# Local attention's product with V in four tiles of 64x64, its result in two banks, and one plain copy of the turned weights

## What is computed

```
bq = q.reshape(b, h, nw, w, d)                  # w = 32, nw = 8 windows, d = 64
bk2, bv2 = (look(bk), look(bv))                 # keys of the window before and of this one: 64
mask = (it < jb) | (it > jb + w) | (jb == -1)
sim = jnp.einsum('bhwie,bhwje->bhwij', bq, bk2) * QK_SCALE
sim = jnp.where(mask, -jnp.finfo(sim.dtype).max, sim)
attn = jax.nn.softmax(sim, -1)
out = jnp.einsum('bhwij,bhwje->bhwie', attn, bv2)
```

## Time and profile before

| | us |
|---|---|
| median of three runs | 1871.23 |
| lowest and highest | 1869.65, 1872.12 |
| the profiled execution's own time | 1873.87 |
| its span, first to last instruction | 1872.1 |

### The profile page before, as it was taken

The page is one execution under the profiler, slowest core; times in us unless marked ns, Lnnn a source line. Parts: engine busy times, 40 slices in busy tenths (PEclk is TensorE's granted clock), DMA queues, the critical chain, the costliest instruction groups (busy, mean ns, idle before and its releaser), DMA issues.

```text
span 1872.1 us, 67927 instructions
## 1 busy us (share of the span) xinstructions
PE 1808.1 (97%) x26763; PEld 1370.4 (73%) x26763; DVE 1535.6 (82%) x3002; ACT 1456.2 (78%) x2976; POOL 1359.4 (73%) x1165
## 2 busy tenths in 40 slices
PE   6999998999999999999999999999999999999997
PEld 4777776777777777777777777777777777777774
DVE  5776777788889888888888888888888888888886
ACT  5766665678798888888887888778878878887884
POOL 3010023889889888888888898888888888888880
PEclk9999999999999999999999999999999999999999
DMA  3000001344343444334444434443344434444342
GB/s 111 1 1 0 0 25 28 91 114 116 104 110 100 112 113 111 97 103 110 114 112 104 105 102 115 113 107 101 103 106 122 112 98 103 111 104 103 98 103 69
DMA packets 200545, 171.01 MB, mean 91 GB/s; under 512 B 32400, under 2 KB 199480, under 8 KB 200248
## 3 DMA queue, kind: packets, MB, share of 16 engines
q1 hardware_dynamic: 200248, 166.89, 34.1%
HBM read 21.01 MB, written 1.05 MB: 12 GB/s over the span
## 4 chain that ended last, share of the span: by engine, by line
PE 61%; ACT 12%; DVE 11%; issue 7%; SPq 5%; POOL 4%; DMA 1%; ACTq 0%; DVEq 0%; POOLq 0%
PE bank L1011 6%; PE bank L1052 6%; PE bank L979 5%; PE pair_bank L1030 5%; PE bank L1062 4%; SPq L366 4%; PE bank L1114 3%; PE bank L1063 3%; PE bank L1064 3%; PE bank L1040 3%; PE bank L1136 3%; PE bank L897 2%; ACT sq L656 2%; DVE rot_v L1378 2%; PE bank L985 1%
## 5 line engine op out<-in xcount | busy, mean ns | idle before, releaser
L437 POOL TENSOR_TENSOR z_norm<-probs_t,z_raw 128x512 f32<-128x512 f32 x376 | 480.9, 1279 | 106.4 <-DVE probs_t L1459 104.2
L443 POOL TENSOR_TENSOR z_raw<-rot_u,rot_v 128x512 f32<-128x512 f32 x384 | 497.9, 1301 | 74.8 <-DVE rot_v L1378 72.0
L1377 DVE TENSOR_TENSOR rot_u<-bank,tabs 128x512 f32<-128x512 f32 x384 | 263.2, 685 | 175.8 <-ACT sq L656 174.6
L1062 PE MATMUL bank<-x_high,w_high 128*128 128x256 f32 x768 | 302.2, 394 | 0.0
L470 POOL TENSOR_TENSOR sqs<-sq 128x512 f32<-128x512 f32 x192 | 246.3, 1283 | 59.0 <-issue 57.9
L1378 DVE TENSOR_TENSOR rot_v<-bank,tabs 128x512 f32<-128x512 f32 x384 | 261.3, 681 | 0.0
L1052 PEld LDWEIGHTS bank<-probs_t,v_late 128*64 128x64 f32 x3072 | 155.0, 137 | 144.4 <-issue 144.4
L732 ACT ACTIVATE pair_bank<-pair_bank 128x512 f32<-128x512 f32 x192 | 111.7, 582 | 169.9 <-DVE pair_bank L1358 168.5
L656 ACT ACTIVATE sq<-bank 128x512 f32<-128x512 f32 x384 | 222.0, 593 | 24.2 <-PE bank L1064 17.7
L665 ACT ACTIVATE probs_t<-bank 64x512 f32<-64x512 f32 x340 | 200.9, 591 | 22.8 <-PE bank L1040 20.7
L1064 PE MATMUL bank<-x_low,w_high 128*128 128x256 f32 x768 | 216.4, 282 | 0.0
(11 more groups left out here) (190 smaller groups left out, 4538.6 us busy)
## 6 DMA issues: line engine op xcount, KB each, us to landing
zqk<-z_norm SPq DMA_DIRECT2D x1536, 64.0 KB, 2.1
v_late<-v_sb SPq DMA_DIRECT2D x192, 192.0 KB, 2.6
w_stage<-in_L_ffn_Wqkv SPq DMA_DIRECT2D x24, 384.0 KB, 3.6
v_late<-v_sb SPq DMA_DIRECT2D x192, 32.0 KB, 2.8
wo<-in_L_ffn_Wo SPq DMA_DIRECT2D x24, 128.0 KB, 2.4
w<-in_L_ffn_W SPq DMA_DIRECT2D x12, 170.5 KB, 3.1
z_norm<-in_L_attn_x SPq DMA_DIRECT2D x4, 256.0 KB, 5.3
out<-z_raw SPq DMA_DIRECT2D x4, 256.0 KB, 2.3
```

Of the source, the lines that this page charges most:

```text
L437: return pool.tensor_tensor(z_norm[:, parity, idx, :, :], rinv(m)[:, idx, :].unsqueeze(1).broadcast_to([P, 2, T]), z_raw[:, parity, idx, : ...
L443: pool.tensor_tensor(z_raw[:, parity, idx, :, :], rot_u[:, idx, :, :], rot_v[:, idx, ::-1, :], ALU.add).then_inc(S[mark], 1)
L1062: pe.matmul(dst, w_high[:, r, j, cols], x_high[:, odd, :], start=True, stop=False)
L1377: dve.tensor_tensor(rot_u[:, idx, :, :], src, tabs[:, 2 * idx, :, :], ALU.mult)
```

## The change

- `spread` has 128 columns a head in place of 256, with no zeros. POOL's clearing of it goes, and `spread_out` becomes one copy of 128x512, on ACT and in kind 1 on DVE.
- `weigh_windows` makes for each head and tile two matmuls of 64 rows by 64 columns with 32 moving columns, one for the upper and one for the lower rows, in four tiles of the array (row half x, column half a). 32 matmuls a slot in place of 16. Results of the upper rows go to bank 2, those of the lower rows to bank 4, the queries' bank, in its first 256 columns.
- So the product now also waits until the last queries are taken from bank 4 (`q_prod`, `q_square`), and `queries` waits until ACT has copied the lower rows' results out of it (`lyt_half`).
- `output_out` becomes two copies of 128x256: that of bank 4 between Ln and Exp of the norms, that of bank 2 at its old place.
- In kind 0 the values are projected ahead of the queries, and ACT takes the values out ahead of the queries' squares.

```diff
-        spread = probs_t...[:, 0:HG * TILES * KEYS].rearrange("p (h s c) -> p h s c", h=HG, s=TILES)
+        spread = probs_t...[:, 0:HG * P]
...
-                tiles = B_T.rearrange("p (h s c) -> p h s c", h=HG, s=TILES)
-                for x in range(2):
-                    rows = slice(KEYS * x, KEYS * x + KEYS)
-                    a = act.activation(spread[rows, :, :, WIN * x:WIN * x + WIN], tiles[rows, :, :, :], ACT.Copy)
-                a.then_inc(S["spread_ready"], 1)
+                act.activation(spread[:, :], B_T[:, :], ACT.Copy).then_inc(S["spread_ready"], 1)
...
-            def output_out(n):
+            def output_half(n, x, mark):
...
-                act.activation(yt[:, 2 * og:2 * og + 2, :], B_T.rearrange("p (c t) -> p c t", c=2), ACT.Copy).then_inc(S["lyt_ready"], 1)
+                dst = yt[:, 2 * og:2 * og + 2, :].rearrange("p c (t x k) -> p c t x k", t=TT, x=2)[:, :, :, x, :]
+                act.activation(dst, B_PV[x][:, 0:T].rearrange("p (c t k) -> p c t k", c=2, t=TT), ACT.Copy).then_inc(S[mark], 1)
...
+                after(pe, "lyt_half", m - 4)
                 project(m, 0, B_Q, m // G % 2, "lq_done", ("q_prod", "q_square"))
...
-                for pair, tile, a in itertools.product(range(2), range(TILES), range(2)):
+                after(pe, "q_prod", min(n + 5, GROUPS))
+                after(pe, "q_square", min(n + 5, GROUPS))
+                for pair, tile, x, a in itertools.product(range(2), range(TILES), range(2), range(2)):
                     h, t = 2 * pair + a, tile // 2
-                    y = B_T[D * a:D * a + D, T * pair:T * pair + T].rearrange("p (t x s c) -> p t s x c", t=TT, x=2, s=2)
-                    mm = pe.matmul(y[:, t, tile % 2, :, :], (v_sb if tile % 2 else v_late)[:, odd, t, f], spread[:, h, tile, :], start=True, stop=True,
-                                   tile_position=(0, D * a), skip_group_check=True)
+                    f, rows = slice(g * GW + h * D, g * GW + (h + 1) * D), slice(KEYS * x, KEYS * x + KEYS)
+                    at, of = P * pair + KEYS * t + WIN * (tile % 2), P * h + WIN * tile
+                    mm = pe.matmul(B_PV[x][D * a:D * a + D, at:at + WIN], (v_sb if tile % 2 else v_late)[rows, odd, t, f], spread[rows, of:of + WIN],
+                                   start=True, stop=True, tile_position=(KEYS * x, D * a), skip_group_check=True)
...
-                if one:
+                if one and mlp_slot(s, 16):
+                    values(s + 4, (s + 4) // G % 2)
                     queries(s + 4)
-                if one:
+                elif one:
+                    queries(s + 4)
                     values(s + 4, (s + 4) // G % 2)
```

More of the change, by code:

```diff
@@ L160, in build @@
         scored = probs.rearrange("p h c -> p (h c)")[:, 0:HG * 2 * KEYS].rearrange("p (a k r) -> p a k r", a=2, r=KEYS)
-        spread = probs_t.rearrange("p h c -> p (h c)")[:, 0:HG * TILES * KEYS].rearrange("p (h s c) -> p h s c", h=HG, s=TILES)
+        spread = probs_t.rearrange("p h c -> p (h c)")[:, 0:HG * P]
         late_ln = probs.rearrange("p h c -> p (h c)")[:, 2 * GW * 2:].rearrange("p (a t) -> p a t", a=2)
@@ L189, in build @@
         B_T, B_M, B_X = bank[2], bank[3], bank[6]
+        B_PV = (bank[2], bank[4])
         both = pair_bank[:, :, 0:4 * KEYS].rearrange("p a (k r) -> p a k r", r=KEYS)
@@ L201, in build @@
             n_done ln_done rinv_ready bound_ready zn_ready z_in0 z_in1 z_in2 z_in3 lv_ready v_late_in0 v_late_in1 v_late_in2 v_late_in3
-            scores_done mask_laid top_ready shifted raised sum_ready part_ready weights_ready turned spread_ready lpv_done lyt_ready
+            scores_done mask_laid top_ready shifted raised sum_ready part_ready weights_ready turned spread_ready lpv_done lyt_half lyt_ready
             wo_in0 wo_in1 wo_in2 wo_in3 lwo_done lres_done xc_done xc_ready xc_squared var_done ln_var rstd_ready xh_raw xh_ready
@@ L454, in slot @@
                 one, two = active(s, -4, GROUPS - 4), active(s, -3, GROUPS - 3)
-                if s == 0:
-                    pool.wait_ge(S["pv_done"], STEPS)
-                    pool.memset(spread[:, :, :, :], 0.0).then_inc(S["spread_zero"], 1)
                 if one:
@@ L722, in slot @@
                 if s == 1:
-                    act.wait_ge(S["spread_zero"], 2)
+                    act.wait_ge(S["pv_done"], STEPS)
                 if four and not mlp_slot(s, 17):
@@ L736, in slot @@
                     act.activation(ln_n(m), B_N[:, :].rearrange("p (a t) -> p a t", a=2), ACT.Ln, bias=tiny[:, 0:1], scale=LNS).then_inc(S["ln_done"], 1)
+                if four:
+                    output_half(s - 1, 1, "lyt_half")
+                if two:
                     act.wait_ge(S["ln_done"], m + 1)
@@ L740, in slot @@
                 if four:
-                    output_out(s - 1)
+                    output_half(s - 1, 0, "lyt_ready")
                 early = s % (2 * G) == 1 and active(s, 0, GROUPS - 1)
@@ L763, in slot @@
                     rotary_part(l, 1, 0)
+                if mlp_slot(s, 16) and active(s + 1, -3, GROUPS - 3):
+                    values_out(s + 4)
                 if one:
@@ L773, in slot @@
                 if mlp_slot(s, 16):
-                    if active(s + 1, -3, GROUPS - 3):
-                        values_out(s + 4)
                     gelus((s - 16) // (2 * G))
@@ L831, in _ @@
             deviations(W - 1, B_M)
-            output_out(N)
+            output_half(N, 1, "lyt_half")
+            output_half(N, 0, "lyt_ready")
             gained(W - 1)
@@ L1083, in slot @@
                 if s == 1:
-                    pe.wait_ge(S["spread_zero"], 2)
+                    pe.wait_ge(S["spread_zero"], 1)
                 if four:
@@ L1218, in _ @@
             pe.wait_ge(S["q_square"], GROUPS)
+            pe.wait_ge(S["lyt_half"], GROUPS)
             for c in range(3):
@@ L1346, in spread_out @@
                 after(dve, "lpv_done", n)
-                tiles = B_T.rearrange("p (h s c) -> p h s c", h=HG, s=TILES)
-                for x in range(2):
-                    rows = slice(KEYS * x, KEYS * x + KEYS)
-                    a = dve.tensor_copy(spread[rows, :, :, WIN * x:WIN * x + WIN], tiles[rows, :, :, :])
-                a.then_inc(S["spread_ready"], 1)
+                dve.tensor_copy(spread[:, :], B_T[:, :]).then_inc(S["spread_ready"], 1)
             def shift_windows(n):
```

1 line of the change is left out of this document (removed).

## The result

| | before | after |
|---|---|---|
| median, four runs each, us | 1870.44 | 1899.31 |
| lowest and highest | 1868.35, 1872.12 | 1898.40, 1902.16 |
| ratio, 95% interval | | 1.0157, [1.014, 1.0175] |
| span of the profiled execution | 1872.1 | 1898.2 |

The forecast was 1902 us, the range 1868 to 1924.

The account below looks back on a forecast made before the run. PE, busy 97%, was taken to bound the kernel, with ACT and DVE waits at slot ends. Product -6, ACT delays +31, slots 1 to 12 +6: +31 us on the 1872.1 span, median 1902 us, range 1868 to 1924.

Parts of the forecast that it names:

- The product: On PE, the load of 64 weight columns sets the pace: 1.06 us, a gain of 0.03 in some 190 slots, -6 us.
- the rivals' 0.77 and 0.55: Product on PE at the scores' pace, 0.77 us (1871 us, chance 0.13), or halved to 0.55 (1850 us, chance 0.09).
- The upper bound of 1.25: Longest product time on PE, if half the 64 instructions come late behind the new wait; whole 1922 us, chance 0.08.
- The delay of ACT's list: Half copy waits for the product's end ahead of Exp, so ACT's later steps come 0.5 us later; +31 us from slot 13.
- kinds 0 to 2 together: ACT's late list delays DVE's hidden values, for which line 1150 waits, so kind 2 ends later: +0.50 us.
- kind 5: Half copy, late behind Ln, delays the second query matmul on PE: +0.17 us.
- kind 6: ACT's gate copy comes 0.42 us later and line 1150 on PE starts later: +0.18 us.
- kind 7: ACT's gate copy comes 0.51 us later, and line 1158 on PE with it: +0.51 us.
- the fourth rival: Half copy from PSUM dearer by 0.06 us each than line 685's from SBUF: +9 us, 1911; chance 0.70 together with the forecast.
- the table load: Sign on ACT: kind 0's table load comes 0.5 us later in its slot.
- The wait of the queries: Queries on PE wait for the half copy; in kind 1 the stall falls into the same 0.5 us and the old wait.
- Slots 1 to 12: No MLP matmul between product and queries, so the wait costs 0.66 us in slot 6: +6 us, between +3 and +8.

Follow-up runs that it names:

- b1: Kernel before, only its output copy cut in two halves, the first between Ln and Exp of the norms; 1890.8 us, ratio 1.0108.
- c1: Changed kernel with bank 4's half copied behind Exp from slot 13 on, except in kinds 1 and 5; 1876.80 us, ratio 1.0042.
- c2: Changed kernel, half ahead of Ln in kinds 1 and 5 (from slot 13), behind Exp elsewhere, values ahead of queries in slots 1 to 12; 1880.84 us.
- b3: Kernel before with only DVE's hidden values moved ahead of the bound of the norms in kind 2; 1862.69 us, ratio 0.9959.
- b2: Kernel before, kind 2's hidden values ahead of the bound, kind 7's variance squares and gate copy ahead of the keys' squares; 1866.88 us, again 1863.94.
- a1: Changed kernel with every product instruction streaming its 32 columns twice, same weight loads; 1901.32 us in a single run.
- a2: Changed kernel with only 32 of V's 64 columns per head loaded as weights, result incomplete; 1864.39 us in a single run.
- d1: Changed kernel, half behind Exp from slot 13 except kinds 1 and 5, plus earlier kind 2 hidden values and kind 7 squares and gate copy; 1869.87 us.
- c3: Changed kernel, half placed by kind, values first in slots 1 to 12, plus earlier kind 2 hidden values and kind 7 squares and gate copy; 1873.67 us.

## Why the prediction was right, step by step

**The product.** Right. Forecast 1.06, measured 1.065; the rivals' 0.77 and 0.55 did not come. The gain over before was sized at 0.03 and is 0.017: over 190 slots 3 us rather than 6. (The upper bound of 1.25 was a slip: 1.06 and the 0.17 allowed are 1.23. Nothing hangs on it.) The Trainium skill ("TensorEngine Tiling (Array Packing)", Theoretical Speedup) gives up to twice the speed for 64 rows or columns; the trace has 1.082 to 1.065 us.

**The delay of ACT's list.** Right in mechanism: b1, with this edit alone, makes 0.94 of the 1.03 us. Against my figures, where the third column takes off the product's gain of 0.03 in a slot, which the lengths of the slots contain:

| term, us | forecast | with the product's gain | after | b1 (no gain) |
|---|---|---|---|---|
| kinds 0 to 2 together | +0.50 | +0.41 | +0.39 | +0.31 |
| kinds 3 and 4 together | 0 | -0.06 | 0 | -0.02 |
| kind 5 | +0.17 | +0.14 | +0.10 | +0.07 |
| kind 6 | +0.18 | +0.15 | +0.15 | +0.19 |
| kind 7 | +0.51 | +0.48 | +0.40 | +0.39 |
| sum | +1.36 | +1.12 | +1.04 | +0.94 |

The terms that were too large are those of kinds 5 and 7. The half copy takes 0.383 us and not 0.42, and the next step starts 0.26 to 0.28 behind its start and not 0.31 (1110.08, 1110.36; 1165.63, 1165.91). I had priced it by line 685, which reads SBUF, and set as the fourth rival that from PSUM it would be dearer; it is cheaper. In kind 5 I had the second query matmul 6.28 behind the slot's start, by way of Ln. The timeline of PE in slot 101, which starts at 1145.02, has it at 6.07, no later than before's 6.11:

```profile
1150.84 0.42 PE L1064 MATMUL bank<-x_high,w_high 128*128 128x256 f32 x1
1151.09 0.28 PE L1065 MATMUL bank<-x_high,w_low 128*128 128x256 f32 x1
```

ACT did there what was forecast, but a little faster at each step, and one slot is not the kind: over 22 slots it is +0.10.

The claims on the table load (0.5 later, measured 0.32) and on PE ahead of 1162 in kind 7 (idle for 0.5, bracket 0.31) are too large as well. ACT's busy time fell by 102 us, more than the 40 asked for, and its wait for DVE ahead of the exponentials grew by 101.

**The wait of the queries.** I had said that it costs nothing of its own in kinds 0 to 2, since it falls into the old wait for the hidden values. It fits the table of waits (12.7 us new, of the old 8.0 only 1.7 left), and c1 against c2 have the same sum of kinds 0 to 2 with the stall and without it in kind 1.

**Slots 1 to 12.** Forecast +6, measured +2.6, just under the 3 of its range. I had carried the 0.66 of slot 6 to nine slots. In eight of them (1, 3, 4, 5, 7, 8, 11 and 12) the cost is 0.23 to 0.55, mostly 0.44 (7.10 us in place of 6.66), 3.4 together; slots 2, 6, 9 and 10, which hold single waits of before or after, come to -0.8. In b1 the twelve cost 1.2, which is no more than two traces of one kernel differ.

**What I had not in the sum.** Slots 189 to 191 are 2.5 us longer, where I had 0.86 for them as the last kinds 5 to 7. Their products take 1.61, 2.14 and 1.06 us (last section). The part behind slot 191 is 1.5 us shorter, which I had at nothing; it goes with the clock (above). So the sum of +31 against a measured +26 of span is the slots 13 to 188 at 24.6 against 22.7, slots 1 to 12 at 6 against 2.6, and these two, +0.8 against +1.0 together. That the last two, neither foreseen, cancel is luck, and so is a part of how close the whole came: the product's gain was 3 us too large and the terms against it were too large as well. The order of ACT's list, the term that carries the forecast, is shown by b1 and c1.

**Kind 2's stall.** I took the 0.39 us ahead of line 1150 in before as given and only asked how it would move. It was a matter of order on DVE: the hidden values stood behind the bound of the norms, the trace of before has both, and b3, five runs, shows that to swap them is worth 7.7 us; b2, with the same swap, has 4.8 and 6.9.

## What to carry over

Smaller tiles save what is streamed, not what is loaded: find by the first instruction behind a pause, or by halving one of the two, which of them sets the pace, before the tiles are made. In a list worked off in order, a step that waits for another engine, put ahead of one that used to run inside that wait, makes the whole list late by about its own length, and the cost shows where a slot already ends on that engine's result. Before a new order is tried, look at each end of a slot that waits and ask whether the step it waits for could stand one place earlier.

## What the runs showed of the hardware

- **Loads in tiles.** An instruction with 64 weight columns goes every 0.058 us in its tile, with 32 moving columns (after) as with 64 (before, a1), with 64 rows as with 128. Four tiles do so side by side. With 32 weight columns the whole product takes 0.687 us.
- **A product that runs dry.** In slots 189 to 191 of after PE stood in the middle of a product, with no other instruction or engine as the cause ("issue"). The timeline of PE in slot 190:

```profile
1859.19 0.29 PE L1054 MATMUL bank<-probs_t,v_sb 64*64 64x32 f32 x6
1860.33 0.19 PE L1054 MATMUL bank<-probs_t,v_sb 64*64 64x32 f32 x1 [0.84 <-issue]
```

These three slots take 1.6 to 2.7 us more than before's in a1, a2, c1 and d1 as well, and nothing more in c2 and c3, which have the same product and the same 80594 instructions. The instructions' own transfers grew from 3.38 to 4.18 MB with after's longer program (queue 8, "instruction"):

```profile
q8 instruction: 255, 4.18, 1.0%
```

The clock does not make the gap: in a1 PE's granted clock is full from 20.5 to 1880.8 us, and slot 190 (from 1855.6) has a gap of 1.40 all the same. In after it is full from 337.3 up to 1863.0, behind the gap of 0.84, and then 1.2 GHz for 3.4 us. That stretch has a price of its own. In a1 and c1, which have none in slots 189 to 191, these slots are no more longer (2.7 and 1.8 us) than their products are (2.8 and 2.2). In after and d1, which have one there, they are 2.5 and 2.6 longer and their products only 1.6 and 1.4: some 1 us goes with the clock, as an estimate from these four. Whether the instructions come too slowly in the gap was not tried; its cause stays open.
- **A copy of 256 columns from PSUM on ACT** takes 0.383 us and lets the next step start 0.27 behind its start, one of 512 columns 0.58 and 0.48: two halves cost ACT's list 0.06 more than the whole.
